# Expert results: gathered at the end, or added to the output tile by tile

## The reference, cut to what matters

```python
xn = _layernorm(x, axis=-1)
x = x + _L1_gnn_ref(xn, ...) + _L1_mix_ref(xn[None], ...)[0]      # "x3" in the kernel
f = _layernorm(x, axis=-1)[None]
rh = relu(f @ router_w1 + router_b1)
expert_logits = softmax(rh @ router_w2 + router_b2, axis=-1)         # 6 experts
top_w, top_i = lax.top_k(expert_logits, 2)
routing_weights = softmax(top_w, axis=-1)                            # the row's two shares
h1 = relu(einsum('bsd,edh->bseh', f, expert_w1) + expert_b1)
h2 = relu(einsum('bseh,ehf->bsef', h1, expert_w2) + expert_b2)
expert_out = einsum('bsef,efo->bseo', h2, expert_w3) + expert_b3
sel = take_along_axis(expert_out, top_i[:, :, :, None], axis=2)
x = x + sum(sel * routing_weights[..., None], axis=2)
```

## Time and profile before

| | us |
|---|---|
| median of 3 runs (lowest, highest) | 6405.18 (6404.75, 6407.28) |
| span of the profiled execution; no other time of it is known | 7249.7 |
| router stage, from the second pair on to the last Pool stores | about 6535 to 6784 |
| expert stage, first turn to last y | 6788.6 to 7093.5 |
| gathers and additions at the end | 7093.5 to 7249.7 |

### The profile page before, as it was taken

The page is one execution under the profiler, slowest core; times in us unless marked ns, Lnnn a source line. Parts: engine busy times, 40 slices in busy tenths (PEclk is TensorE's granted clock), DMA queues, the critical chain, the costliest instruction groups (busy, mean ns, idle before and its releaser), DMA issues.

```text
span 7249.7 us, 87859 instructions
## 1 busy us (share of the span) xinstructions
PE 5328.2 (73%) x24977; PEld 4445.0 (61%) x24977; DVE 3382.5 (47%) x9891; ACT 1308.8 (18%) x2962; POOL 3860.9 (53%) x4349
## 2 busy tenths in 40 slices
PE   0111110667659999999899999979999899997794
PEld 0000000556537777777678887868788778876682
DVE  8511100666645555555464464436444554446323
ACT  0000000111101111111142242214111231111240
POOL 0777776000055555555888888830666326654205
PEclk9755555778779999999999999989999999999895
DMA  1000000221133333335310011021333223353223
GB/s 37 9 12 12 12 12 11 73 66 58 59 105 98 96 99 100 98 97 93 49 48 18 14 40 34 20 70 48 91 95 97 76 71 107 108 93 109 89 94 117
DMA packets 319771, 477.56 MB, mean 66 GB/s; under 512 B 99008, under 2 KB 240054, under 8 KB 319470
## 3 DMA queue, kind: packets, MB, share of 16 engines
q0 software_dynamic: 153136, 262.81, 14.8%
q1 hardware_dynamic: 166334, 211.17, 9.5%
HBM read 371.27 MB, written 102.33 MB: 65 GB/s over the span
## 4 chain that ended last, share of the span: by engine, by line
PE 57%; another core or an unknown queue 13%; DVE 11%; issue 11%; DMA 4%; DVEq 2%; ACT 1%; SPq 1%; POOL 1%; ACTq 0%; POOLq 0%
PE bank L2277 13%; PE bank L2288 13%; PE bank L2505 5%; PE bank L2338 5%; PE bank L2487 4%; PE bank L2323 4%; PE bank L2774 3%; PE bank L2630 2%; PE bank L2268 2%; PE bank L2816 1%; DMA sb_work_QT<-scratch_q 1%; DMA sb_rows<-scratch_xn,sb_row_of 1%; DMA sb_work_XC<-in_x 1%; DVE sb_STATE L1391 1%
## 5 line engine op out<-in xcount | busy, mean ns | idle before, releaser
L995 POOL DMA_INDIRECT sb_rows<-scratch_xn,sb_row_of x1760 | 1718.7, 977 | 1553.2 <-PE bank L2323 619.1
L988 POOL DMA_INDIRECT scratch_sorted<-sb_FREE x1564 | 1589.6, 1016 | 546.5 <-issue 379.2
L2288 PE MATMUL bank<-sb_work_FT,sb_W 128*128 128x250 f32 x4400 | 1006.9, 380 | 19.6 <-ACT sb_work_FT L1075 15.1
L2288 PEld LDWEIGHTS bank<-sb_work_FT,sb_W 128*128 128x128 f32 x4400 | 845.3, 193 | 134.6 <-ACT sb_work_FT L1075 22.0
L1075 ACT ACTIVATE sb_HT<-bank,sb_cols 128x250 f32<-128x250 f32 x1333 | 552.8, 467 | 2047.2 <-PE bank L2487 811.6
L2277 PE MATMUL bank<-sb_W,sb_HT 128*125 128x256 f32 x4000 | 894.2, 380 | 1.1 <-ACT sb_HT L1075 1.1
L2277 PEld LDWEIGHTS bank<-sb_W,sb_HT 128*125 128x125 f32 x4000 | 752.7, 188 | 115.4 <-ACT sb_HT L1075 1.9
L2277 PE MATMUL bank<-sb_W,sb_work_FT 128*125 128x256 f32 x1600 | 409.3, 406 | 449.8 <-issue 378.3
L2277 PEld LDWEIGHTS bank<-sb_W,sb_work_FT 128*125 128x125 f32 x1600 | 315.0, 201 | 518.0 <-issue 450.5
L2323 PE MATMUL bank<-sb_rows,sb_work_TM 128*125 128x257 f32 x1760 | 444.8, 392 | 91.2 <-issue 29.7
L1660 DVE TENSOR_TENSOR sb_FREE<-sb_FREE,bank 125x257 f32 x440 | 186.1, 423 | 698.0 <-PE bank L2323 455.1
(11 more groups left out here) (375 smaller groups left out, 7606.2 us busy)
## 6 DMA issues: line engine op xcount, KB each, us to landing
sb_rows<-scratch_xn,sb_row_of POOLq DMA_INDIRECT x1760
scratch_sorted<-sb_FREE POOLq DMA_INDIRECT x1564
scratch_qT<-sb_work_QF SPq DMA_DIRECT2D x100, 250.0 KB
sb_work_QF<-scratch_qT SPq DMA_DIRECT2D x100, 250.0 KB
sb_work_XC<-in_x SPq DMA_DIRECT2D x50, 250.0 KB
sb_work_ZT<-scratch_xn SPq DMA_DIRECT2D x50, 250.0 KB
sb_W<-in_L_mix_W SPq DMA_DIRECT2D x9, 1024.0 KB
sb_work_XC<-scratch_zs SPq DMA_DIRECT2D x28, 256.0 KB, 2.6
```

The source lines that it names most:

```text
L988: nc.gpsimd.indirect_dma_start(out=sorted_d[e], out_offset=bass.IndirectOffsetOnAxis(ap=pos[e][0:n, c:c + 1], axis=0), in_=rec[e][0:n, 2 * ...
L995: nc.gpsimd.indirect_dma_start(out=rows[:, t % RING, 0:D], out_offset=None, in_=table, in_offset=bass.IndirectOffsetOnAxis(ap=row_of[:, t: ...
L2288: ins = nc.tensor.matmul(dst[:, b, :], w[:, k0 + k, 128 * (b0 + b):128 * (b0 + b) + 128], source[:, k, :], start=(n == 0), stop=(n == 2 * ...
```

## The change

- Each row of the sorted table `zs` gets five numbers more: the row's number, its two experts and its two shares (DW = 261 in place of 256). DVE writes them into the z buffers (a new small copy, "row", per pair; the others are written there in place of into GATE and OWN). The z buffers move to other SBUF space. A padding row has a row number beyond the output.
- x3 is stored to the output by SP as soon as it is made, in the router stage (`store_x3`, 25 stores that were at the end).
- In the expert stage DVE works out, for the tile two ahead, each row's share for that tile's expert ("shares", "share") and the row's number as an index ("at"), into slots of a ring of four. Before it overwrites a slot it waits until the tile that had it has been added to the output (`result_added`).
- y becomes an addition: bank plus the expert's third bias, which now lies in SBUF on all partitions. ACT then multiplies y by the share, two instructions for the tile's two halves.
- Pool adds the two halves to the output in DRAM by indirect stores with `compute_op=ALU.add`. A tile's two stores wait for ACT's y and for the landing of the stores of the tile before, since a row can stand in tiles of two experts. Row numbers beyond the output are left out.
- `ys`, `place_results`, `place_gates`, the gathers, the bias matmuls and the final additions go.

```diff
-X_ACT = named(2, "turn") + named(1, "a") + named(0, "b")
-X_DVE = named(2, "w0", "bias") + named(1, "w1") + named(-1, "y")
+X_ACT = named(2, "turn") + named(1, "a") + named(0, "b") + named(-1, "y")
+X_DVE = named(2, "w0", "bias", "shares", "share", "at") + named(1, "w1") + named(-1, "y")
 XRING = 4
-YRING = 3
+ROW, OWNER, SHARE, DW = D, D + 1, D + 3, D + 5
...
 # SP, router stage, for pair j
+            def store_x3(j):
+                wait(sp, c1_dve.done("x3", j))
+                for s in slots_of(j):
+                    n = 4 * j + 2 * s
+                    sp.dma_start(tiles(out)[:, n:n + 2, :], XM[:, n:n + 2, :]).then_inc(out_stored, 16)
...
 # SP, expert stage
-            for b in range(-2, NX + 1):
-                t = b + 2
-                if t + XRING < NX:
-                    wait(sp, x_pe.done("turn", t))
-                    load_tile(t + XRING)
-                t = b - 1
-                if t >= 0:
-                    wait(sp, x_dve.done("y", t))
-                    sp.dma_start(by_tile(ys_d)[:, t, :], ...).then_inc(y_stored[t % XRING], 16)
-            for j in range(NC):
-                sp.wait_ge(gate_added, 5 * (j + 1))
-                sp.dma_start(tiles(out)[:, 2 * j:2 * j + 2, :], ...).then_inc(out_stored, 16)
+            for t in range(NX - XRING):
+                wait(sp, x_pe.done("turn", t))
+                wait(sp, x_dve.done("at", t))
+                load_tile(t + XRING)
             sp.wait_ge(out_stored, 16 * NC)
+            sp.wait_ge(result_added, 32 * NX)
...
 # Pool, after the stores of zeros
-            for j in range(NC):
-                if j >= YRING:
-                    pool.wait_ge(gate_added, 5 * (j - YRING + 1))
-                for t in range(2):
-                    for k in range(2):
-                        nc.gpsimd.indirect_dma_start(out=GY[j % YRING][:, t, k, :], in_=ys_d, ...)
+            pool.wait_ge(out_stored, 16 * NC)
+            for t in range(NX):
+                q = t % XRING
+                wait(pool, x_dve.done("at", t))
+                wait(pool, x_act.done("y", t))
+                if t:
+                    pool.wait_ge(result_added, 32 * t)
+                hold(pool)
+                for u in range(2):
+                    nc.gpsimd.indirect_dma_start(
+                        out=out, out_offset=bass.IndirectOffsetOnAxis(ap=OUT_AT[:, q, u:u + 1], axis=0),
+                        in_=YB[q][:, u, :], in_offset=None, bounds_check=N - 1, oob_is_err=False,
+                        compute_op=ALU.add).then_inc(result_added, 16)
...
 # ACT, expert stage, last in round b
+                t = b - 1
+                if t >= 0:
+                    wait(act, x_dve.done("y", t))
+                    for u in range(2):
+                        ins = move(YB[t % XRING][:, u, :], YB[t % XRING][:, u, :], scale=SHAREOF[...])
...
 # DVE, expert stage, round b, t = b + 2, behind the biases
+                    q = t % XRING
+                    dve.wait_ge(tile_loaded[q], 16 * (t // XRING + 1))
+                    if t >= XRING:
+                        dve.wait_ge(result_added, 32 * (t - XRING + 1))
+                    nc.vector.scalar_tensor_tensor(SHARES[:, q], XB[q][:, :, OWNER:OWNER + 2], exp_all[:, t:t + 1],
+                                                   XB[q][:, :, SHARE:SHARE + 2], ALU.is_equal, ALU.mult)
+                    wait(dve, x_dve.done("shares", t))
+                    nc.vector.tensor_reduce(SHAREOF[:, q], SHARES[:, q], AX.X, ALU.add)
+                    nc.vector.tensor_copy(OUT_AT[:, q], XB[q][:, :, ROW])
                 if 0 <= b + 1 < NX:
                     take_weights(b + 1, 1)
                 t = b - 1
                 if t >= 0:
                     wait(dve, x_pe.done("c", t))
-                    if t >= XRING:
-                        wait(dve, (y_stored[t % XRING], 16 * (t // XRING)))
-                    nc.vector.tensor_copy(YB[t % XRING], PSUMS[t % 2]...)
+                    nc.vector.tensor_tensor(YB[t % XRING], PSUMS[t % 2]..., bexp1[...], ALU.add)
```

More of the change, by code:

```diff
@@ L111 @@
 C1_DVE = (named(1, "x3", "stats", "mean") + named(0, "logit", "lmax", "lsub") + named(1, *RSQRT)
-          + named(0, "lsum", "lrec", "p", "max", "arg", "argf", "one", "pair", "gdif") + named(1, "z")
+          + named(0, "lsum", "lrec", "p", "max", "arg", "argf", "one", "pair", "gdif") + named(1, "row", "z")
           + named(0, "gsum", "g1", "g2", "at", "prod", "pos", "index", "add", "acc"))
 TILE = 256
-CAP = TILE * ((N + 2 * TILE - 1) // TILE)
+CAP = TILE * ((N + 2 * TILE - 1) // TILE + 1)
 CAP_TILES = CAP // TILE
@@ L486, in build @@
         ACC, CAPS, ADD = (carve(8, T) for _ in range(3))
-        ZR = [QT, [tok(W0[:, 1024:2048].rearrange("p (s n) -> p s n", s=2), s) for s in range(2)],
-              [tok(HT[:, :, 4:8, :].rearrange("p s b n -> p s (b n)")[:, :, 0:2 * D], s) for s in range(2)]]
+        wide_ht = HT[:, :, :, :].rearrange("p s b n -> p (s b n)")
+        wide_rows = rows[:, :, :].rearrange("p q n -> p (q n)")
+        ZR = [x[0:T, at:at + 4 * DW].rearrange("p (t n) -> p t n", t=4)
+              for x, at in ((wide_ht, CH), (wide_ht, 9 * CH), (wide_rows, 0))]
         ZN = len(ZR)
@@ L564, in build @@
         z_scattered = [sem(f"z_scattered_{q}") for q in range(ZN)]
-        tile_loaded, y_stored = ([sem(f"{n}_{q}") for q in range(XRING)] for n in ("tile_loaded", "y_stored"))
-        y_gathered = [sem(f"y_gathered_{q}") for q in range(YRING)]
+        tile_loaded = [sem(f"tile_loaded_{q}") for q in range(XRING)]
+        result_added = sem("result_added")
         pads_scattered, pads_ready = sem("pads_scattered"), sem("pads_ready")
         route_step, route_sums = sem("route_step"), sem("route_sums")
[L569 to L572, removed]
+        out_stored, routing_cleared = sem("out_stored"), sem("routing_cleared")
         ROUTE_STEPS = ["tiles", "whole", "began", "ended", "done", "row", "real", "in", "rel", "in0",
-                       "last", "exp_of", "in_of"]
+                       "last", "exp_of", "in_of", "exp_all"]
         def route(step):
@@ L886, in load_xn1 @@
                 sp.dma_start(ZT[s], tiles(xn1_d)[:, n:n + 2, :]).then_inc(xn1_read[s], 16)
+            def store_x3(j):
[3 more added lines that the diff above has]
+                    sp.dma_start(tiles(out)[:, n:n + 2, :], XM[:, n:n + 2, :]).then_inc(out_stored, 16)
             for s in range(2):
                 load_xn1(0, s)
-            load("exp_up", (bexp1, a["L1_ffn_expert_b3"]), *[expert(0, e) for e in range(NEXP1)])
-            sp.wait_ge(routing_cleared, 8)
+            load("exp_up", *[expert(0, e) for e in range(NEXP1)])
+            sp.wait_ge(routing_cleared, 9)
             for j in range(NP):
@@ L1055, in _ @@
                         in_=zero_rows, in_offset=None).then_inc(pads_scattered, 16)
[L1056 to L1059, removed]
-            for j in range(NC):
-                if j >= YRING:
-                    pool.wait_ge(gate_added, 5 * (j - YRING + 1))
-                    hold(pool)
-                for t in range(2):
-                    for k in range(2):
-                        nc.gpsimd.indirect_dma_start(
-                            out=GY[j % YRING][:, t, k, :], out_offset=None, in_=ys_d,
-                            in_offset=bass.IndirectOffsetOnAxis(ap=Y_AT[:, 2 * j + t, k:k + 1], axis=0))\
-                            .then_inc(y_gathered[j % YRING], 16)
+            pool.wait_ge(out_stored, 16 * NC)
[11 more added lines that the diff above has]
+                        compute_op=ALU.add).then_inc(result_added, 16)
         @block.scalar
@@ L1274, in _ @@
                     relu_tile(b, "b", H2, PC, 1)
[L1276 to L1281 removed]
+                t = b - 1
+                if t >= 0:
+                    wait(act, x_dve.done("y", t))
+                    for u in range(2):
+                        ins = move(YB[t % XRING][:, u, :], YB[t % XRING][:, u, :], scale=SHAREOF[:, t % XRING, u:u + 1])
+                    ins.then_inc(*x_act.add("y", t))
         @block.vector
@@ L2065, in body_c1 @@
                 at, ch = 4 * j, 4 * (j + 1)
+                z = ZR[j % ZN]
                 lg = LG4[:, 0:n, 0:NEXP1]
@@ L2165, in _ @@
             dve.wait_ge(route_sums, 3)
-            step("row", nc.vector.tensor_copy(exp_row, EXPERT))
+            step("row", nc.vector.tensor_copy(exp_row, EXPERTS[0:1, :]))
             step("real", nc.vector.tensor_scalar(real, exp_row, NEXP1 - 0.5, None, ALU.is_lt))
```

143 lines of the change are left out of this document (45 added, 98 removed).

## The result

| | median of the runs | lowest to highest | profiled execution: span |
|---|---|---|---|
| before | 6406.01 us (4 runs) | 6404.75 to 6407.28 | 6406.1 us (taken anew, below) |
| after | 6451.36 us (4 runs) | 6445.1 to 6458.59 | 6447.5 us |

The ratio is 1.0071, with a 95% interval of 1.0056 to 1.0085: slower by 0.7%, or 45 us. The time lies in the range given (6325 to 6485), but on the other side of no change from the forecast of 6380.

A forecast was written before the change was run, and what follows sets the result against it. PE was taken to bound the expert tiles (5.62 us each), Pool the 156 us tail. With serial rounds the span ends at 7212, 38 us earlier; -38 + 2 + 10 = -26 gives about 6380 us, range 6325 to 6485.

The forecast's parts named there:

- The tail: Gathers and additions behind the expert tiles: 156 us removed, some 20 not Pool's, half of those counted as saving.
- The chain: Expert tiles: landing, DVE, ACT, Pool's start and two stores in a row, a round of 7.9 us per tile.
- Pool's first store: 0.95 and the gap of 0.30: In each expert tile's round: the first store's issue and the gap, so that the second begins at 4.5 us.
- a dearer issue: Accumulating stores in expert tiles: costlier issue, covered with the read by 1.0 us added to the landing time.
- L = 3.4: Expert tiles: from the second accumulating store's beginning to its landing, 3.4 us, within bounds of 2.40 to 5.11.
- the last three rounds: Last three expert tiles: no such wait on DVE, they follow by Pool alone, each 2.05 us plus the landing time.
- The turning point: Whole kernel: time 6199.3 + 53 times the landing time, even with before at a landing of 3.88 us.
- Rival 2: Expert tiles: accumulating store dear in issue or on DMA engines; 6470 us at the landing's upper bound; chance 0.34.
- Rival 1: Expert tiles: the store lands almost as a plain one, 2.4 to 3.0 us; 6327 us at 2.4; chance 0.15.
- Rival 3: Expert tiles: TensorE's clock falls; at 1.2 GHz throughout, 11.2 us of PE per tile, some 6550 us; chance 0.05.
- Rival 4: Expert tiles: stores don't hold up y, Pool's 5.45 us alone serial, PE's 5.62 bound; 6255 us; chance 0.03.
- Ring or not, everything from landing to landing is in a row: Expert tiles: y waits for the previous tile's stores and its own stores for y, a round of 7.9 us.

The follow-up runs named there:

- the second profile: The kernel before, unchanged, profiled once more to get an execution that is not stretched: 6407.95 us.
- The second experiment: The kernel after with its 108 indirect stores writing in place of adding: 6352.00 us, 0.9917 of before.
- the fifth experiment: The kernel after with only the first of each tile's two accumulating stores, half of the rows left out: 6351.26 us, 0.9912 of before.
- The third experiment: The kernel after with DVE's shares, row numbers and their wait for the stores moved behind w1 and y, all work done: 6337.79 us, 0.9892 of before.
- the fourth experiment: The kernel after with eight buffers instead of four for shares and row numbers, the wait for the stores moved to y alone: 6353.81 us, 0.9914 of before.
- the sixth experiment: The kernel after with both accumulating stores over 64 of 128 partitions, half of the rows left out: 6412.74 us, 1.0011 of before.

## Why the prediction was right in the mechanism and wrong in the sign

**The tail.** Of its 156 us, 20 were taken not to be GpSimd's, and half of them as missing in the runs. In the second profile 16.3 of them are missing. The saving was 139.9 us, not the 146 of the sum: 6 us too much.

**The chain.** The order was right: 50 times DVE waits at L2210 for a landing, and y, ACT and GpSimd follow in turn. The parts of the round that rested on rows of the same operation came out: DVE, ACT and GpSimd's start were put at 3.25 us, and the chain has 3.3 (landing at 6153.64 + 3.81 = 6157.45, store at 6160.71). The two terms for the accumulating store failed.

- "Pool's first store: 0.95 and the gap of 0.30". The issue takes 1.55 us. The 0.95 is the duration of a gather and of a plain store of 128 rows; I carried it over to an operation that the trace didn't show, without a bound, though I had bounded the landing. The prediction did allow for "a dearer issue", but only in the 1.0 us added to L, where the second store's issue runs beside its landing; the first store's stands in the round by itself. That is 0.60 us in every round, the larger half of the miss. The second experiment has 0.97 for the plain form.
- "L = 3.4". Measured 3.6 to 3.8 in the chain and 3.8 at the median, inside the bounds of 2.40 and 5.11. I had chosen the end of the range that is nearer to a plain store, whose 2.40 the second experiment has again. That is some 0.35 us a round.

Together the round is 8.9 in place of 7.9: 50 of them lie between the first store, at 5973.8, and the one at 6418.52, so (6418.5 - 5973.8) / 50 = 8.89. By the sum's own form, the 49 full rounds cost 48.5 us more than forecast. Three smaller terms add to it: there are 54 tiles and 108 stores, not the 53 and 106 that the description ahead of the prediction gives and the sum went by (one more round, 8.9 us); the last three rounds, GpSimd's alone, took 18.7 us in place of 16.4; and the program ends 10.3 us behind the last tile's first store, where a landing was counted (4.7). In all 65 us, and 6 for the tail; the router stage gives some 5 back (2 us counted for its copies were not lost, and y begins 2.9 us earlier; both may be the difference between two executions). From -26 that makes +40; the two profiled spans differ by 41.4, the medians of the runs by 45.

**The turning point.** The prediction said that a tenth of a microsecond of the round stands 53 times, and that the change turns to a loss from L = 3.9. L is below that. But the dearer issue works as L does, so that the L of its formula is 3.72 (the mean of the two in the chain) + 0.60 = 4.32, and 6199.3 + 53 x 4.32 = 6428. The other 23 us are in the main the extra tile (8.9), the tail (6), the end (about 5 more than this L accounts for) and a round of 8.89 in place of 8.82 (3 to 4); the 5 us of the router stage and the 4 by which spans and medians differ nearly cancel.

**The rivals.** Rival 2, the dear accumulating store "in its issue or on the DMA engines", is what happened, with both of its places. Against it I had set only its upper bound, a second DMA in the landing, and called that far off; the first store's issue had no price of its own. Rival 1 is what the second experiment shows when the addition is left out: 6352, not 6327, chiefly for the smaller terms named. Rival 3: the granted clock did fall, from 1.00 to 0.89, but PE isn't late for y (12.0 us in four waits). In the second and the fifth experiment PE was busy 242 and 241 of the 288 us and the clock was 1.00; in after it was busy 218. Rival 4, that the stores don't hold up y, was rightly set aside for this kernel. The third experiment makes it true, and there GpSimd's own part is 6.6 us, where I had put 5.45, for the most part by the same two terms. "Ring or not, everything from landing to landing is in a row" doesn't hold without its condition: in the fourth experiment, with eight slots and the wait at y alone, the round is 6.83 us.

The Trainium skill (DMA: Bandwidth & Descriptors, Anatomy of one DMA — SWDGE (gpsimd) path) gives a fixed 2.0 us and the bytes at 436 GB/s; with a read counted as well that was the estimate of 2.6 us in the prediction. The plain stores agree with the rule, 2.40 measured against 2.3. The accumulating ones do not: 3.8. The measurement decides; an addition in the store isn't priced by its bytes alone. The same section of the Trainium skill calls the generation of descriptors small and slow to grow with their number. If that is what GpSimd does in an issue, which no run shows, the sixth experiment agrees as to the number, 0.13 us for 64 rows more; that the form of the operation adds 0.58 us at the same number of rows stands in the runs alone.

## What to carry to other kernels

When work from a parallel tail is put into a loop, look first for what in the loop waits for its end: here one wait ahead of w1 and y made a store that could have run beside PE into a serial round, and moving it behind them on the same engine turned a loss of 0.7% into a gain of 1.1%. An operation that the trace doesn't show needs a bound on every resource that it takes, its issue as well as its landing; the duration of its plain form was only a lower bound here (0.97 against 1.55 us), not an estimate. And a profile whose span is 13% above the runs should be taken again before a stretch of it is used as a saving.

## What the runs showed of the hardware that was not expected

- An accumulating indirect store of 128 rows of 1 KB takes 1.55 us of GpSimd and 3.8 us to landing, a plain one 0.97 and 2.4. It makes three times the packets (142 against 48) and three times the engine time (18.6 us against 5.8) on the DMA engines.
- Half of its rows cost nearly the same issue (1.42 us) and 3.1 us to landing.
- In after, two accumulating stores 1.85 us apart don't lengthen each other: a single one lands in 3.8 us too (fifth experiment).
- GpSimd's start behind a semaphore is 0.8 us behind ACT (after) and 0.9 behind a landing (fourth experiment), as before (0.74 and 0.89), and stands in every round.
